# A gated-slot attention step: turning the previous step's outputs behind the value projection instead of ahead of it

## What is computed

```
q, k, v = heads(xn @ Wq), heads(xn @ Wk), heads(xn @ Wv)     # 16 heads: 64, 64, 128 wide
s = clip(heads(xn @ Ws), -32, 32)                            # 64 slots per head
z = cumlogsumexp(s);  g = exp(z_prev - z);  p = exp(s - z)
hk = hk * g + k p^T;  ok = q . hk                            # scan over time
pv = softmax(ok)
hv = hv * g + p v^T;  ov = pv . hv                           # scan over time
o = ov * rsqrt(mean(ov^2) + eps) * g_norm_weight
x = x + (o * silu(xn @ Wg)) @ Wo
```

## Time and profile before

| | us |
|---|---|
| median of 3 runs | 2103.16 |
| lowest and highest | 2103.12, 2106.79 |
| the profiled execution | 2105.88 |
| its span | 2104.1 |
| TensorE busy in the span | 1841.9 (88%) |
| VectorE, ScalarE, GpSimd busy | 1371.7, 847.8, 828.3 |

### The profile page before, as it was taken

How to read it: one execution, slowest core, us unless ns; L and a number is a source line. 1 busy time by engine, 2 the same in 40 slices (tenths; PEclk the granted TensorE clock), 3 DMA queues, 4 the chain that set the end, 5 groups by cost and what they waited for, 6 DMA issues and landing times. The chain is left out here.

```text
span 2104.1 us, 39769 instructions
## 1 busy us (share of the span) xinstructions
PE 1841.9 (88%) x13586; PEld 1547.6 (74%) x13587; DVE 1371.7 (65%) x2986; ACT 847.8 (40%) x2008; POOL 828.3 (39%) x1165
## 2 busy tenths in 40 slices
PE   5999999999999999982699999999999967749990
PEld 3788788887888778871388888888888845647870
DVE  5766676667666677766766766666776647514445
ACT  3434443444433443431355555555555531213330
POOL 3332432333332432334443444444443324636661
PEclk9999999999999999995699999999999957969995
DMA  2100010000950000000110010010000051366655
GB/s 89 46 0 0 0 46 0 0 0 20 357 4 0 1 1 0 0 0 8 63 41 0 1 41 0 0 41 0 0 1 0 0 197 52 103 167 192 191 174 219
DMA packets 72760, 108.20 MB, mean 51 GB/s; under 512 B 24988, under 2 KB 53980, under 8 KB 72028
## 3 DMA queue, kind: packets, MB, share of 16 engines
q1 hardware_dynamic: 62300, 77.38, 12.7%
q0 software_dynamic: 9216, 25.44, 3.3%
q10 hardware_dynamic: 1152, 4.19, 0.5%
HBM read 62.17 MB, written 45.09 MB: 51 GB/s over the span
## 5 line engine op out<-in xcount | busy, mean ns | idle before, releaser
L1394 POOL TENSOR_TENSOR b_rot<-b_by_cos,b_by_sin 128x512 f32<-128x512 f32 x128 | 164.8, 1287 | 363.0 <-DVE b_by_sin L1296 359.3
L791 POOL TENSOR_TENSOR a_ms<-a_ms,a_esq 128x4 f32<-128x4 f32 x64 | 12.7, 199 | 469.4 <-DVE a_ms L691 469.4
L1872 POOL DMA_INDIRECT ys<-m_yb,m_dest x128 | 122.8, 959 | 85.1 <-issue 68.4
L680 DVE TENSOR_TENSOR a_mix_m<-a_ps_av,square_consts 128x512 f32<-128x512 f32 x64 | 44.3, 692 | 121.9 <-PE a_ps_av L432 121.9
L1254 ACT ACTIVATE b_prob<-b_sc,b_nmax 128x128 f32<-128x128 f32 x256 | 99.7, 391 | 52.6 <-DVE b_nmax L1338 52.6
L598 DVE RECIPROCAL a_rz<-a_ps_sz 128x256 f32<-128x256 f32 x64 | 112.5, 1758 | 3.4 <-PE a_ps_sz L344 3.4
L557 ACT ACTIVATE a_sq<-a_ps_og 128x512 f32<-128x512 f32 x64 | 38.2, 597 | 175.8 <-PE a_ps_og L452 160.4
L691 DVE TENSOR_REDUCE a_ms<-a_sq 128x4 f32<-128x512 f32 x64 | 43.9, 685 | 86.8 <-ACT a_sq L557 86.8
L1145 PE MATMUL b_ps_o<-b_pT,b_V 128*128 128x64 f32 x512 | 100.0, 278 | 0.0
L1145 PE MATMUL b_ps_o<-b_pT,b_Vs 128*128 128x64 f32 x512 | 96.6, 271 | 0.7 <-ACT b_pT L1227 0.7
L1308 DVE TENSOR_TENSOR b_oT_lo<-b_ps_o,b_oT_hi 128x512 fp32r<-128x512 f32 x64 | 44.3, 692 | 67.1 <-ACT b_oT_hi L1232 67.1
(11 more groups left out here) (344 smaller groups left out, 6321.6 us busy)
## 6 DMA issues: line engine op xcount, KB each, us to landing
xs<-a_zeros SPq DMA_DIRECT2D x32, 528.0 KB, 14.4
m_xb<-xs SPq DMA_DIRECT2D x32, 528.0 KB, 4.2
wgu_all<-wgu SPq DMA_DIRECT2D x4, 2048.0 KB, 14.3
m_wd<-wd SPq DMA_DIRECT2D x2, 2048.0 KB, 17.5
f_got<-ys SPq DMA_DIRECT2D x8, 512.0 KB, 14.3
f_got<-ys ACTq DMA_DIRECT2D x8, 512.0 KB, 14.3
X<-x SPq DMA_DIRECT2D x2, 1024.0 KB, 7.2
a_w_raw<-Wv SPq DMA_DIRECT2D x4, 512.0 KB, 6.4
```

The source lines that it names most:

```text
L680: nc.vector.tensor_tensor(pairs(mix_m[:, b, :, :]), ps_as, tri.unsqueeze(1).unsqueeze(1).broadcast_to([P, 2, 2, P]), ALU.mult).then_inc(c[ ...
L1394: nc.gpsimd.tensor_tensor(rot[:, i, :, :], by_cos[:, i, :, :], by_sin[:, i, :, :], ALU.add)\
L1872: pool.indirect_dma_start(ys, bass.IndirectOffsetOnAxis(ap=dest[:, i % RING, j:j + 1], axis=0), yb[:, i % RING, j // 2, j % 2, :], None).t ...
```

## The change

In `step` of TensorE, the call of `turn_o` for step H - 1 moves from in front of the value projection of step H + 1 to behind it. It stays ahead of the first half of the gate projection. The other engines' programs are the same.

```
                 last.then_inc(c["p_ok"], 1)
+                if nxt:
+                    project(H + 1, n, "v", group_next)
                 if prev:
                     turn_o(H - 1, n)
                 if nxt:
-                    project(H + 1, n, "v", group_next)
                     project(H + 1, n, "g", group_next, range(1))
```

## The result

The changed kernel takes 2192.22 us (median of 4 runs, 2191.89 to 2193.28), the kernel before, on the same chip, 2104.59 us (2103.12 to 2106.79): 1.0416 times as long, 95% interval 1.0403 to 1.043, or 88 us more. The forecast was 2194 us, between 2180 and 2214.

What follows compares the result with a forecast made beforehand. TensorE was taken to bound the kernel, with L363's delay reaching L410 through ScalarE's queue. The terms 79.0 + 7.6 + 4.3 = 91 us, put on the median of 2103.16, gave 2194 us, range 2180 to 2214.

Steps and rivals of the forecast that it cites:

- not slower: Rival: L542 is set by VectorE's subtraction alone, so L410 stays and the time is 2101 us; chance 0.03.
- 52 ordinary steps: Gated-slot steps where L410 starts later by L363's whole delay: 1.52 us each, 79.0 us.
- 7 first steps of a group: Steps where L363 already waited for a_o, so the V block partly fills that gap: 1.09 us each, 7.6 us.
- 3 changeovers: Steps at changeovers of the weights: two at 1.52 us, one at 1.25 with TensorE at low clock, 4.3 us.
- last step: Step 63 of the gated-slot stage: it has no projection, so it was left out of the delayed steps.
- The allowance for the change from fp32r to f32 work: Extra delay in front of L363 on TensorE from a second change of kind: 0 to 0.10 us a step.
- The chain from L513 to L410: Distance of 2.04 us in two differing steps, taken to show that this chain already releases L410.
- the 0.1 us of slack that was read: Slack of ScalarE's queue at L542, which VectorE's subtraction kept waiting; about 0.1 us and no more.
- The lower bound of 1.30 us a step: Low end of the range: 0.17 us a step given back by a quicker L542 or L671; 77 us, 2180 us.
- The clock did not fall: Rival: TensorE's new gap lowers its clock, 2235 us for half the steps, 2276 for all; chance 0.09 for many steps.
- the price read from one changeover (1.33): Cost of one clock fall on TensorE: L396 to L410 took 5.52 us in one changeover, 4.19 in another.
- given back at L396: Rival: TensorE's 20 us wait at L396 doesn't follow TensorE and vanishes under the delay, 2174 us; chance 0.06.

Runs made afterwards that it cites:

- half_v: Kernel before with the turn of the outputs between the two halves of the V projection: 2257.02 us against 2214.43 for the kernel before in its set.
- late_g: Changed kernel with the turn of the outputs also behind the first three gate matmuls: 2401.36 us against 2216.61 for the kernel before in its set.
- a_esum_first: Changed kernel with ScalarE's copy esum_hi ahead of the copy oT_hi: 2274.21 us against 2214.43 for the kernel before in its set.
- a_exp_then_sum: Changed kernel with ScalarE's order exponential, esum_hi, oT_hi: 2204.74 us against 2216.61 for the kernel before in its set.
- after_again: The changed kernel run once more, unaltered: 2302.09 us against 2216.61 for the kernel before in its set.
- b_exp_first: Kernel before with ScalarE's order esum_hi, exponential, oT_hi: 2237.86 us against 2214.43 for the kernel before in its set.
- b_exp_then_sum: Kernel before with ScalarE's order exponential, esum_hi, oT_hi: 2206.48 us against 2216.61 for the kernel before in its set.

## Why the prediction was right, point by point

**The bound and the chain.** That TensorE bounds the stage and that L363's delay reaches it through ScalarE's queue was right: the delay arrives in full when the queue has L513 ahead of both esum_hi and the exponential (half_v, late_g), less when only the exponential stands behind it (a_esum_first), and not at all when it is turned round (a_exp_then_sum, where the turn stands just as late). The rival "not slower" named the condition for this, ScalarE taking the exponential ahead of L513; with that order the move is free.

**The sizes.** By the spacing of the turns of w_ in the two traces:

| term | predicted, us | measured, us |
|---|---|---|
| 52 ordinary steps | 79.0 (1.52 each) | 72.9 (1.40 each) |
| 7 first steps of a group | 7.6 (1.09) | 6.8 (0.97) |
| 3 changeovers | 4.3 | 6.1 (2.90, 1.61, 1.57) |
| last step | 0 | 0.8 |
| sum | 91 | 86.5 |

The second trace of the changed kernel (after_again) gives 73.1, 6.7, 6.2 (3.2, 0.3 and 2.8) and 0.0: the ordinary steps repeat, the single changeovers and the last step do not.

The term of the ordinary step was 0.12 us too large. The V block took the 1.47 us that was read (340.09 - 338.62). The allowance for the change from fp32r to f32 work, 0 to 0.10 us, is 0: 340.09 - 339.85 = 0.24, a plain pitch. V starts 0.36 us behind L398's group where L363 had started 0.39 behind, and from L363 to the copy on ScalarE are 0.63 instead of 0.67 us: 1.47 - 0.03 - 0.04 = 1.40. The trace before had shown 0.33 us from a matmul of 512 columns to L432 and was the wrong neighbour: there the weight load sits idle for 0.36 us and starts with L432, while that of L363 lies beside the last V matmul, which starts at 339.85 (first row before, second row after):

```profile
318.60 0.53 PEld L432 LDWEIGHTS a_ps_av<-a_wT,a_eT 64*128 64x128 f32 x8 [0.36 <-issue]
```

```profile
339.86 0.59 PEld L363 LDWEIGHTS a_ps_og<-square_consts,a_o 128*128 128x128 f32 x4
```

Why L432's comes late is open: both lines stand behind a semaphore that had long been given, and L432 differs by its weights of 64 rows; no run separates these. Here the Trainium skill ("TensorE: Matmul & The Clock Gate", section "Part 2: What happens when you issue a matmul") has the rule that a weight load is pulled ahead of a matmul under way; the row of L363 agrees. Its figure of 216 ns for a matmul of 512 columns, weighed in the prediction, would have given 1.30 us for the block; the rows of before and after both show 1.47.

The changeovers were too small by 1.8 us: 1.3 of that is one more fall of the clock, in the first of them. The two errors went against each other in part; the sum is still 4.4 us too large. That the forecast of 2194 us lies within 2 us of the measured time is luck: the kernel before has a median 1.4 us higher with the later runs than the one that the forecast was put on, and the runs differ by 87.6 us, 1.1 more than the turns in the two traces.

**The chain from L513 to L410**, 2.04 us before, is 342.75 - 340.72 = 2.03 us after. The number was right, and its use too; the path that holds it constant is not the one that the prediction took. Two instructions that feed L410 stand behind L513, esum_hi and the exponential, and the prediction followed the exponential alone. The one that sets L410's start is esum_hi (L538): GpSimd's esum_lo starts 0.49 us after L538 starts, and L671 ends 1.02 us after esum_lo starts. The rows were in the trace of the kernel before, step 19:

```profile
315.44 0.74 POOL L775 TENSOR_TENSOR a_esum_lo<-a_esum,a_esum_hi 128x256 fp32r<-128x256 f32 x1 [0.49 <-ACT a_esum_hi L538]
...
315.82 0.64 DVE L671 TENSOR_TENSOR a_w<-a_prob,a_rz 128x256 f32<-128x256 f32 x1 [0.49 <-ACT a_prob L542]
```

315.82 + 0.64 = 316.46, and 315.44 + 1.02 = 316.46. In the changed kernel the exponential is only 1.30 us later against the subtraction (1.33 instead of 0.03), since it does have the 0.1 us of slack that was read; L671 takes 0.74 us instead of 0.64, and together that is the 1.40 of the step. This distance of 1.02 us is there in 61 of 64 steps before and 63 of 64 after. Both instructions follow L513 in the queue, so the two paths give the same price to within 0.1 us a step. That the slack took nothing off is owed to esum_lo, which the prediction did not have. The lower bound of 1.30 us a step had reckoned with a quicker L671, and a_esum_first shows that this is there to be had, but only when esum_lo moves.

**The rivals.** The clock did not fall in ordinary steps. That a gap of 2.1 us brings falls (36 of 62) at 1.5 us each is shown by late_g, that one of 1.4 us brings none by the changed kernel; the price read from one changeover (1.33) was a little low. Nothing was given back at L396: 20.2 us before and after.

## What to carry to other kernels

Before work is moved behind other work on a busy engine, look at who reads its result, and what stands behind that reader in the reader's queue: here a copy that nobody was in a hurry for stood ahead of two instructions that TensorE waits for by way of VectorE and GpSimd, and there was no slack to pay for the move. A distance between two instructions that stays equal in steps which differ otherwise marks a chain that binds, and a change can be priced by it; which path holds it equal is a question of its own. When the order on an engine is changed, ask also what it lets start earlier on GpSimd, and which VectorE operation runs at that time.

## What the runs showed of the hardware

VectorE and GpSimd held each other up. A VectorE operation on 128x256 with both inputs in SBUF (L666, L671) takes 0.42 to 0.43 us alone. When GpSimd's L775 (two SBUF inputs, 0.73 to 0.75 us) has started first, it ends some 1.02 us behind GpSimd's start, though its own start differs: 308.81 + 1.02 = 309.83 against 308.80 in b_exp_first, 341.96 + 0.74 = 342.70 against 341.69 in the changed kernel. That is 0.28 us behind GpSimd's end. So it is held until GpSimd is through; why 0.28 us and not the whole 0.42 are left then, no row shows. When VectorE is first, GpSimd is the one that takes longer; step 0 of the kernel before (VectorE, then GpSimd):

```profile
47.87 0.43 DVE L671 TENSOR_TENSOR a_w<-a_prob,a_rz 128x256 f32<-128x256 f32 x1 [0.49 <-ACT a_prob L542]
47.95 0.93 POOL L775 TENSOR_TENSOR a_esum_lo<-a_esum,a_esum_hi 128x256 fp32r<-128x256 f32 x1
```

Where GpSimd starts 0.34 us behind L671, in b_exp_then_sum, neither is longer. The reduction L674, with one input, keeps its 0.41 us beside the same GpSimd operation (b_exp_then_sum: 0.413 mean). The Trainium skill, "SBUF — State Buffer", section "Who interferes with whom", says just this: an operation of VectorE with two SBUF inputs and one of GpSimd that reads SBUF exclude each other, whoever comes first; one with a single input, outside the modes that use both ports, does not. The traces agree. It was not used in the prediction, and was what made the first turned-round order 23 us slower instead of 8 us faster.

The granted clock went to its lower level behind 36 of the 62 idle stretches of TensorE of 2.07 to 2.15 us in late_g, and behind 20 of the 39 stretches of 1.7 us at L396, three in each of the thirteen traces. It did behind none of the 61 stretches of 1.4 us in the changed kernel, and again none of 61 in after_again. The length of the stretch alone does not decide it; what else does, these runs leave open.
